# Embedding dimensions transposed three at a time, and layer 0's x0 read from SBUF, in a CIN recommender kernel

## The reference, cut to what matters

```python
e = stack([tbl_f[ids[:, f]] for f in range(39)], axis=1)   # 1024 x 39 x 16
x0 = xk = e
for idx, (W, b) in enumerate([(w0, b0), (w1, b1), (w2, b2)]):   # W: 39 x fields of xk x 128
    z = relu(einsum('bhd,bkd,hks->bsd', x0, xk, W) + b[None, :, None])
    if idx != 2:
        xk = z[:, :64, :]; direct.append(z[:, 64:, :])
    else:
        direct.append(z)
z = sum(concatenate(direct, axis=1), axis=-1)              # 1024 x 256
h = concatenate([z, dense_ctx], axis=1)
h = maximum(h @ W_top1 + b_top1, 0); h = maximum(h @ W_top2 + b_top2, 0)
y = h @ W_top3
```

## Time and profile before

| | |
|---|---|
| median of 3 runs | 1267.36 us |
| the profiled execution | 1268.23 us, span 1266.4 us |
| PE | 1231.7 us busy, 4256 instructions |
| DVE | 1165.7 us, 1045 |
| ACT | 707.7 us, 741 |
| POOL | 900.8 us, 569 |
| DMA | 234.42 MB, mean 185 GB/s |
| granted TensorE clock, mean over the span | 0.984 |

### The profile page before, as it was taken

How to read it: one execution, slowest core, us unless ns; L and a number is a source line. 1 busy time by engine, 2 the same in 40 slices (tenths; PEclk the granted TensorE clock), 3 DMA queues, 4 the chain that set the end, 5 groups by cost and what they waited for, 6 DMA issues and landing times.

```text
span 1266.4 us, 15522 instructions
## 1 busy us (share of the span) xinstructions
PE 1231.7 (97%) x4256; PEld 783.5 (62%) x4256; DVE 1165.7 (92%) x1045; ACT 707.7 (56%) x741; POOL 900.8 (71%) x569
## 2 busy tenths in 40 slices
PE   4879999999999999999999999999999999999999
PEld 2446666666666666666666666666666666666664
DVE  7479999989999999999999999999999999999991
ACT  1245655556565655556655655557555565565552
POOL 7676777876878787787877778787878755654540
PEclk7789999999999999999999999999999999999999
DMA  7699878777998888888988888889888888897510
GB/s 210 151 167 222 202 180 187 180 196 191 219 213 178 185 190 197 201 200 210 215 178 185 192 193 201 203 210 219 177 181 195 194 200 198 206 219 174 134 51 0
DMA packets 135922, 234.42 MB, mean 185 GB/s; under 512 B 16403, under 2 KB 25101, under 8 KB 135787
## 3 DMA queue, kind: packets, MB, share of 16 engines
q1 hardware_dynamic: 84335, 151.67, 52.1%
q10 hardware_dynamic: 41994, 79.99, 24.8%
q0 software_dynamic: 9568, 2.47, 2.1%
HBM read 230.21 MB, written 6.23 MB: 187 GB/s over the span
## 4 chain that ended last, share of the span: by engine, by line
PE 83%; DMA 5%; DVE 4%; POOL 3%; SPq 2%; issue 2%; ACT 1%; DVEq 0%; ACTq 0%; POOLq 0%
PE z_odd L1041 33%; PE z_even L1041 31%; PE z_even L1075 7%; PE z_odd L1075 6%; DMA x_rep<-x_rows 2%; DVE whole L889 2%; DMA x_shift<-x_rows 2%; POOL rest L583 2%; PE whole_psum L1069 1%; DVE whole_psum L889 1%; PE x_odd L1095 1%; POOL gathered L568 1%; PE x_even L1095 1%; SPq L441 1%; DVE rest L906 1%
## 5 line engine op out<-in xcount | busy, mean ns | idle before, releaser
L583 POOL TENSOR_TENSOR rest<-whole,head 128x1024 fp32r<-128x1024 f32 x256 | 611.2, 2398 | 247.8 <-ACT head L701 247.2
L889 DVE TENSOR_TENSOR whole<-x_banks,x_rep 128x1024 f32<-128x1024 f32 x448 | 534.1, 1216 | 35.7 <-ACT x_banks L659 30.7
L701 ACT CAST head<-whole 128x1024 fp32r<-128x1024 f32 x256 | 268.6, 1049 | 159.0 <-DVE whole L889 120.7
L568 POOL DMA_INDIRECT gathered<-in_tbl,idx x299 | 286.7, 959 | 82.2 <-issue 74.1
L701 ACT CAST head<-whole_psum 128x1024 fp32r<-128x1024 f32 x192 | 194.8, 1015 | 142.0 <-DVE whole_psum L889 135.8
L889 DVE TENSOR_TENSOR whole_psum<-x_banks,x_rep 128x1024 f32<-128x1024 f32 x192 | 235.5, 1226 | 5.8 <-DMA x_rep<-x_rows 3.5
L906 DVE TENSOR_TENSOR rest<-whole_psum,head 128x1024 fp32r<-128x1024 f32 x192 | 234.5, 1222 | 0.3 <-ACT head L701 0.3
L1041 PE MATMUL z_odd<-head,w_rest 128*128 128x512 f32 x427 | 198.0, 464 | 3.9 <-POOL rest L583 3.3
L1041 PE MATMUL z_even<-head,w_rest 128*128 128x512 f32 x405 | 186.3, 460 | 1.0 <-DVE rest L906 0.8
L1041 PE MATMUL z_odd<-whole,w_whole 128*128 128x512 f32 x400 | 185.3, 592 | 0.5 <-DVE whole L889 0.5
L1041 PE MATMUL z_odd<-head,w_head 128*128 128x512 f32 x460 | 182.5, 397 | 0.0
(11 more groups left out here) (117 smaller groups left out, 1001.5 us busy)
## 6 DMA issues: line engine op xcount, KB each, us to landing
x_rep<-x_rows ACTq DMA_DIRECT2D x128, 512.0 KB, 11.7
x_rep<-x_rows SPq DMA_DIRECT2D x128, 512.0 KB, 11.7
x_shift<-x_rows SPq DMA_DIRECT2D x93, 546.0 KB
x_rep<-x_rows ACTq DMA_DIRECT2D x32, 384.0 KB
x_rep<-x_rows SPq DMA_DIRECT2D x32, 384.0 KB
x_rep<-x_rows SPq DMA_DIRECT2D x32, 256.0 KB
gathered<-in_tbl,idx POOLq DMA_INDIRECT x299, 7.0
x_rows<-xt_and_ctx SPq DMA_DIRECT2D x32, 78.0 KB
```

Source lines behind the costliest of these rows:

```text
L568: nc.gpsimd.indirect_dma_start(gathered[:, f, :], None, tables[f], bass.IndirectOffsetOnAxis(ap=idx[:, f:f + 1], axis=0)).then_inc(s_gathe ...
L583: nc.gpsimd.tensor_tensor(rest[:, split_slot(product)], whole_slot(product), head[:, split_slot(product)].bitcast(F32), ALU.subtract).then ...
L701: nc.scalar.copy(head[:, split_slot(product)], src).then_inc(s_head, 1)
L889: nc.vector.tensor_tensor(out[0:rows, 0:width, :], xk[0:rows, :].unsqueeze(1).to_broadcast([rows, width, N]), x0, ALU.mult).then_inc(s_pro ...
```

## The change

Only dimensions per transpose, and what follows from it, change; the sums are the same.

- From the second block on, ACT writes `emb` once instead of three times, with the dimensions outside and the fields inside (128 x 624). Three dimensions of 39 fields, 117 columns side by side, are one transpose. A block has six: dimensions 0-2, 3-5, 6-8, 9-11, 12-14, and 13-15 again for the last. Its four tiles issue 2, 1, 1 and 2 of them. All go to bank 0; PE waits for ACT's last copy out of it.
- ACT copies 117 rows and 128 or 256 columns into `turned`, three slots of 128 columns in the free part of `emb`.
- SP stores `x_rows` dimension by dimension: eight DMAs a tile with rows of 128 values, of which only the last stands behind the wait for layer 0.
- The bank now holds three dimensions of one copy, and no longer three copies of the fields. Layer 0's three copies come from DRAM: SP loads `x_rows` rows 0 to 38 three times into `x0_rows`, also in the free part of `emb`, behind the loads of `x_shift`. DVE's products of layer 0 read `x0_rows` from tile 3 on and wait for the loads instead of ACT's copy.
- ACT waits for the stores once a set of loads that includes group 0 and no longer before each.

```diff
+DIM_GROUPS = ((0, 1), (2,), (3,), (4, 5))
+FIRST_DIM = (0, 3, 6, 9, 12, 13)
...
+        emb_by_dim = emb[:, 0, :].rearrange("p (d f) -> p d f", f=FIELDS)
+        free_of_emb = emb[:, 1:SPC, :].rearrange("p r q -> p (r q)")
+        x0_rows = free_of_emb[:, 0:N]
+        turned = free_of_emb[:, N:N + SPC * P].rearrange("p (g b) -> p g b", b=P)
...
+        def packed(t):
+
+            return t.turn is not None or t.first >= AHEAD
...
+        def x0_loads(t):
+
+            return t.turn is not None or t.first > AHEAD
...
+                    if packed(t):
+                        for i in range(DPT):
+                            d = nxt.first % TPB * DPT + i
+                            g = min(d // SPC, DIM // SPC - 1) if d < DIM - 1 else DIM // SPC
+                            rows = (d - FIRST_DIM[g]) * FIELDS
+                            slot = turned[:, g % SPC, :]
+                            sp.dma_start(source(row, 0, [[N, FIELDS], [1, P]], i * P),
+                                         slot[rows:rows + FIELDS, :]).then_inc(s_stored, 16)
+                            if i == DPT - 1:
+                                sp.wait_ge(s_prod, before(t, 0, PAIRS0))
+                            sp.dma_start(source(row, FIELDS, [[N, XROWS - FIELDS], [1, P]], i * P),
+                                         slot[rows:rows + XROWS - FIELDS, :]).then_inc(s_stored, 16)
...
+                    if x0_loads(nxt):
+                        for r in range(SPC):
+                            sp.dma_start(x0_rows[FIELDS * r:FIELDS * (r + 1), :],
+                                         source(row, 0, [[N, FIELDS], [1, N]])).then_inc(s_x0_rows, 16)
...
-                act.wait_ge(s_stored, nxt.count(32, 32))
+                if 0 in groups:
+                    wait(act, s_stored, stored(nxt))
...
-                nc.scalar.copy(emb[:], gathered[:].rearrange("p f d -> p (f d)").unsqueeze(1)
-                               .to_broadcast([P, SPC, FIELDS * DIM])).then_inc(s_emb, 1)
+                if is_first(t):
+                    nc.scalar.copy(emb[:], gathered[:].rearrange("p f d -> p (f d)").unsqueeze(1)
+                                   .to_broadcast([P, SPC, FIELDS * DIM])).then_inc(s_emb, 1)
+                else:
+                    nc.scalar.copy(emb_by_dim, gathered[:].rearrange("p f d -> p d f")).then_inc(s_emb, 1)
...
+                if packed(t):
+                    wait(act, s_stored, stored(nxt.plus(-1)))
+                    groups = DIM_GROUPS[nxt.first % TPB]
+                    first, count = groups[0] % SPC, len(groups)
+                    nc.scalar.copy(turned[0:ROWS0, first:first + count, :],
+                                   x0_bank[0][0:ROWS0, 0:count * P].rearrange("p (g b) -> p g b", b=P)
+                                   ).then_inc(s_xt, 1)
+                    return
...
-                    dve.wait_ge(s_xt, nxt.count(1, 1))
+                    if x0_loads(nxt):
+                        wait(dve, s_x0_rows, nxt.count(16 * SPC, -16 * SPC * AHEAD))
+                    else:
+                        dve.wait_ge(s_xt, nxt.count(1, 1))
...
-                            product(t, 0, j, x0_bank[nxt.first % 2], x_shift[0:ROWS0, c, :], ROWS0)
+                            product(t, 0, j, x0_rows if x0_loads(nxt) else x0_bank[nxt.first % 2], x_shift[0:ROWS0, c, :], ROWS0)
...
-                    out = x0_bank[nxt.first % 2]
-                    for i in range(DPT):
+                    if packed(t):
+                        wait(pe, s_xt, nxt.count(1))
+                    out = x0_bank[0 if packed(t) else nxt.first % 2]
+                    for i, g in enumerate(DIM_GROUPS[nxt.first % TPB] if packed(t) else ()):
+                        rows = emb[:, 0, FIRST_DIM[g] * FIELDS:(FIRST_DIM[g] + SPC) * FIELDS]
+                        mm = nc.tensor.transpose(out[0:ROWS0, i * P:(i + 1) * P], rows, ident[:])
```

More of the change, by code:

```diff
@@ L259, in build_kernel @@
         s_xt = sem("xt_ready")
+        s_x0_rows = sem("x0_rows_loaded")
         s_stored = sem("x_rows_stored")
@@ L394, in by_two, with source @@
             return [[0, HALF], [2 * N, repeated(g)], [1, N]]
-        def source(row, first, pattern):
-            return bass.AP(tensor=row.tensor, offset=row.offset + first * N, ap=pattern)
+        def source(row, first, pattern, column=0):
+            return bass.AP(tensor=row.tensor, offset=row.offset + first * N + column, ap=pattern)
         def steps(eng, body, turns=TURNS):
@@ L414, in has_layer0, with stored @@
             return t.turn is not None or -1 <= t.first < TILES - 1
+        def packed(t):
+            return t.turn is not None or t.first >= AHEAD
+        def stored(t):
+            plain = t.turn is None and t.first < AHEAD + 2
+            return t.count(32, 32) if plain else t.count(32 * DPT, -32 * (DPT - 1) * (AHEAD + 2) + 32 * DPT)
+        def x0_loads(t):
+            return t.turn is not None or t.first > AHEAD
         def has_transposes(t):
@@ L534, in body @@
                     wait(sp, s_xt, nxt.count(1, 1))
[L535 to L540, removed]
+                    if packed(t):
[11 more added lines that the diff above has]
+                    else:
+                        now = xt[:, nxt.first % 2, :]
+                        sp.dma_start(source(row, 0, [[N, FIELDS], [1, N]]), now).then_inc(s_stored, 16)
+                        if not first and has_layer0(t):
+                            sp.wait_ge(s_prod, before(t, 0, PAIRS0))
+                        sp.dma_start(source(row, FIELDS, [[N, XROWS - FIELDS], [1, N]]),
+                                     now[0:XROWS - FIELDS, :]).then_inc(s_stored, 16)
                     if first:
@@ L543, in body @@
                         sp.wait_ge(s_prod, before(t, 0, PAIRS0))
-                    wait(sp, s_stored, nxt.count(32, 32))
+                    wait(sp, s_stored, stored(nxt))
                     for r in range(SPC if has_layer0(t) else 0):
@@ L1090, in body @@
                         pe.wait_ge(s_prod, before(t.plus(-1), 0, PAIRS0))
-                    out = x0_bank[nxt.first % 2]
-                    for i in range(DPT):
+                    if packed(t):
[4 more added lines that the diff above has]
+                        mm = nc.tensor.transpose(out[0:ROWS0, i * P:(i + 1) * P], rows, ident[:])
+                    for i in range(0 if packed(t) else DPT):
                         d = nxt.first % TPB * DPT + i
```

## The result

The changed kernel took 1339.04 us (median of 4 runs, 1338.03 to 1340.55) against 1267.83 before: a ratio of 1.0575, with a 95% interval of 1.056 to 1.059. That is 71 us slower, on the side that was forecast and 19 us above the 1320. The profiled execution has a span of 1337.3 us.

The account below looks back on a forecast made before the run. PE bounds the kernel, DVE about 1 us a tile behind. After: DVE 35.07 busy, 0.12 gaps, 2.4 blocked, 0.4 late loads, 38.0 us a tile against 36.16; over 29 tiles 53 us, 1267.4 + 53 = 1320; range 1282 to 1358.

Parts of the forecast that it names:

- DVE blocked once a tile by POOL's rest: Layer 0: POOL's last layer 1 rest gets in behind product 0, and product 1 waits 2.4 us.
- the spare time: DVE's waits for ACT's x1 or x2, which come late because PE does: 0.97 us a tile.
- rival C: Layer 0: DVE keeps POOL out through all four products; 3.0 us a tile, 1354 us; chance 12%.
- Products not shorter from SBUF: Layer 0's products on DVE: two SBUF inputs leave their own length unchanged; the errata's 65 ns each not counted.
- Late loads: SP's queue: three x0 loads ahead of x_rep's groups 2 to 4 cost DVE 0.4 us a tile.
- SP's lead over ACT: x_rep loads: SP's half lands before ACT's, 7.5 against 8.9 us from issue, eating most of the x0 loads' delay.
- Stores at nothing: SP's queue: eight store DMAs a tile fall in its idle time; cost nothing to 0.2 us, zero taken.
- PE's 0.44 worth nothing: Ten fewer transposes a block save PE 0.44 us a tile, worth nothing once DVE is the bound.
- rival A: Layer 0: no blocking, loads covered; PE stays the bound and gives back 12 us, 1255 us; chance 10%.

Follow-up runs that it names:

- The run with 2 columns: The changed kernel, with POOL's last rest of layer 1 subtracting only 2 columns of each chunk: 1272.27 us, 1.0057 to before.
- the run with products 2 and 3: The kernel before, with ACT's copy putting x0 in SBUF; only layer 0's products 2 and 3 read it there, 0 and 1 PSUM: 1265.9 us, 0.9992.

## Why the prediction was right, and which term was too small

- *DVE blocked once a tile by POOL's rest, 2.4 us; 1.44 a tile beyond the spare time, 42 us.* Right in place; the size is partly luck. The four products got 2.19 us longer, and the time 42.1 us with nothing else changed, 41 with all but the loads' place. But with the operand alone DVE's busy time rose by 62.7 us, 2.16 a tile and not 2.4, and its waits for ACT shrank by 25.3, 0.87 a tile and not 0.97; with 0.8 us more of waits for x_rep that is 38 us, and 4 that DVE's waits don't show bring it to 42. POOL got in at the seam behind product 0, as read from the earlier trace rows; had DVE kept it out (rival C), the products would have stayed at 1.22 and the rests grown to 5 or 6. The run with 2 columns shows that it is that one subtraction, the run with products 2 and 3 that it needs both at once.
- The Trainium skill, SBUF — State Buffer, section "Who interferes with whom", says that a DVE instruction with two SBUF inputs contends with a GpSimd one that reads SBUF. Both traces agree: 6.26 us for the four products with POOL's whole rest beside them, 4.09 with 2 columns a chunk. By the same section an instruction on GpSimd that only writes is not held up, and it infers the same for the generation of DMA descriptors. Here gathers went from 0.94 to 1.79 us beside such products, so a gather as a whole is held up. It also reads its indices in SBUF, and no run tells that read from its descriptors.
- *Products not shorter from SBUF.* Right: 678 ns for 117x512 with both inputs in SBUF (29 of them in the kernel with that operand alone), 681 with one in PSUM.
- *Late loads, 0.4 us a tile, 12 us.* This is the term that was mis-sized: 31.4/29 = 1.08 a tile, and all of the 19 us. Two steps of its working failed. SP's lead over ACT was to eat the delay, but ACT's half became the late one: what is added to SP's queue slowed a load in ACT's, by 1.4 to 1.8 us (the run without x0 loads). And the group that is late is 2, the first behind x0, not 4. A third thing was missed: DVE's spare time and the loads' head start are in part the same microsecond. With DVE waiting for x2 after layer 0, x_shift was issued 0.48 us before layer 2 began (603.00 and 603.48), and 0.22 to 0.50 before it in the three tiles that follow. Blocked, DVE goes straight on: x_shift is issued 0.37 us behind (635.61 and 635.24), then 0.16 and 0.51 before and 1.26 behind. I take that for why the same loads cost 5 us with DVE on PSUM and 31 with it blocked; no run tested it by itself.
- *Stores at nothing:* right; beside the loads they even helped.
- *PE's 0.44 worth nothing:* right, and more so than argued. In rival A it was to give 12 us; alone it gave 3, though in the tile measured each transpose fewer gave PE 0.20 us. The spare 0.97 of the earlier trace rows was not the only margin there: the loads had 0.3 us or less.

## What to carry to other kernels

Before an operand of a VectorE instruction is moved from PSUM to SBUF, look in the timeline for a GpSimd instruction that reads SBUF beside it, and charge the whole of it, once for each meeting; here one ScalarE copy back to PSUM took back nearly all. Ask of every load that is added which load stands behind it, in its own queue or beside it in another, and how much margin that has, and put what is needed last behind what is needed first. Where an engine, a load queue and a second engine have all less than a microsecond of margin in a 36 us round, as here, ask how far what is taken off one of them can show: here it was 3 of 12 us.

## What the runs showed of the hardware that was not expected

- POOL's indirect DMA issues wait for a DVE instruction with two SBUF inputs (0.94 us become 1.77 to 1.81), but don't hold it up: four such products beside gathers took 4.09 us.
- 234 KB a tile, 3% of the traffic, in one queue delayed a load in another queue by 1.4 to 1.8 us (in four tiles 12.2, 10.4, 10.0 and 12.1 us with them, 10.4, 9.0, 8.3 and 10.5 without), with the DMA share of these tiles lower than before the change (0.80 against 0.85).
- Eight stores with 512-byte rows instead of two with 2 KB rows cost nothing, and beside extra loads they were worth 23 us, of which the last one's faster landing explains 8 (an estimate, 29 x 0.28).
